# Channel attention of a normalised image batch: norms of queries and keys from weights times T on VectorE, summed by TensorE in fp32

## What is computed

```python
xt = gn(x).reshape(b, c, n).transpose(0, 2, 1)
q, k, v = split(xt @ w_qkv, 3, axis=-1)
q = q / max(sqrt(sum(q * q, over positions)), EPS)
k = k / max(sqrt(sum(k * k, over positions)), EPS) * temperature
attn = softmax(k^T q per head, axis=-1)
out = (v @ attn) @ w_out + b_out
result = x + out
```

## Time and profile before

| | us |
|---|---|
| median of 3 runs | 373.96 |
| profiled execution, its own time | 374.76 |
| span of that execution | 372.8 |
| TensorE busy | 331.2 (89%) |
| VectorE busy | 283.2 (76%) |
| ScalarE busy | 235.9 (63%) |
| POOL busy | 150.4 (40%) |

### The profile page before, as it was taken

The page is one execution under the profiler, slowest core; times in us unless marked ns, Lnnn a source line. Parts: engine busy times, 40 slices in busy tenths (PEclk is TensorE's granted clock), DMA queues, the critical chain, the costliest instruction groups (busy, mean ns, idle before and its releaser), DMA issues.

```text
span 372.8 us, 9327 instructions
## 1 busy us (share of the span) xinstructions
PE 331.2 (89%) x3724; PEld 233.4 (63%) x3724; DVE 283.2 (76%) x666; ACT 235.9 (63%) x410; POOL 150.4 (40%) x133
## 2 busy tenths in 40 slices
PE   0048856999999999999999999999999999999795
PEld 0036645875778566865777577856686577765452
DVE  4889855887699669986799769966998665359774
ACT  1098489763997299747996399729974699610200
POOL 0079858301970169203950197016920395001000
PEclk9999976899999999999999999999999999999999
DMA  7999900004994279815991499427981563034766
GB/s 235 359 286 246 244 16 3 2 2 139 300 323 132 86 233 326 247 44 137 336 335 44 134 297 338 124 87 226 320 261 45 165 217 88 2 105 150 230 213 192
DMA packets 30826, 67.73 MB, mean 182 GB/s; under 512 B 5504, under 2 KB 12096, under 8 KB 30784
## 3 DMA queue, kind: packets, MB, share of 16 engines
q1 hardware_dynamic: 30544, 66.56, 56.7%
q10 hardware_dynamic: 240, 0.59, 0.6%
HBM read 29.38 MB, written 28.31 MB: 155 GB/s over the span
## 4 chain that ended last, share of the span: by engine, by line
PE 64%; ACT 15%; issue 10%; DVE 5%; DMA 2%; SPq 2%; POOL 1%; ACTq 0%; POOLq 0%
PE u_ps L927 30%; PE g_ps L927 17%; PE s_ps L927 10%; ACT h_sb L543 4%; ACT tok L581 4%; ACT xn L537 3%; PE u_ps L976 2%; DMA wo<-in_L_conv_w_out_dram 2%; PE u_ps L977 2%; ACT h_sb L550 1%; DVE x_sb L855 1%; PE u_ps L979 1%; PE u_ps L978 1%; SPq L354 1%; SPq L359 1%
## 5 line engine op out<-in xcount | busy, mean ns | idle before, releaser
L474 POOL TENSOR_TENSOR l_sb<-xn,h_sb 128x768 f16<-128x768 f32 x63 | 103.8, 1649 | 56.0 <-ACT h_sb L543 55.7
L855 DVE SCALAR_TENSOR_TENSOR x_sb<-u_ps,bias,x_sb 128x384 f32<-128x384 f32 x144 | 85.9, 613 | 24.2 <-PE u_ps L927 24.1
L927 PE MATMUL g_ps<-tok 128*128 128x64 f16 (+1 forms) x864 | 87.1, 241 | 3.4 <-ACT tok L581 2.9
L537 ACT ACTIVATE xn<-x_sb,rb 128x768 f32<-128x768 f32 x63 | 63.6, 1020 | 29.7 <-POOL rb L486 29.7
L581 ACT COPY tok<-u_ps 128x384 f32<-128x384 f32 x144 | 65.0, 485 | 19.8 <-PE u_ps L979 18.6
L927 PEld LDWEIGHTS g_ps<-tok 128*128 128x128 f16 x864 | 57.0, 99 | 28.5 <-ACT tok L581 5.8
L728 DVE BATCH_NORM_STATS2 bnst<-x_sb 128x6 f32<-128x384 f32 x144 | 69.9, 543 | 5.3 <-DMA x_sb<-in_x_dram 5.2
L927 PE MATMUL u_ps<-h_sb,ml 128*128 128x384 f16 (+1 forms) x336 | 73.2, 327 | 0.0
L543 ACT ACTIVATE h_sb<-x_sb,rb 128x768 f16<-128x768 f32 x63 | 64.4, 1022 | 0.0
L976 PE MATMUL u_ps<-id,h_sb 128*128 128x128 f16 x288 | 48.9, 223 | 8.2 <-DVE l_sb L718 7.4
L977 PE MATMUL u_ps<-id,l_sb 128*128 128x128 f16 x288 | 48.9, 223 | 0.0
(11 more groups left out here) (144 smaller groups left out, 567.6 us busy)
## 6 DMA issues: line engine op xcount, KB each, us to landing
x_sb<-in_x_dram SPq DMA_DIRECT2D x48, 384.0 KB, 5.4
out_dram<-x_sb SPq DMA_DIRECT2D x48, 384.0 KB, 2.9
out_dram<-x_sb SPq DMA_DIRECT2D x48, 192.0 KB, 2.8
x_sb<-in_x_dram SPq DMA_DIRECT2D x45, 192.0 KB, 5.4
hl<-h_sb SPq DMA_DIRECT2D x48, 96.0 KB, 2.8
hl<-l_sb SPq DMA_DIRECT2D x48, 96.0 KB, 3.0
x_sb<-in_x_dram ACTq DMA_DIRECT2D x3, 192.0 KB, 4.2
w<-in_L_conv_w_qkv_dram SPq DMA_DIRECT2D x1, 288.0 KB, 7.4
```

The lines of the kernel that those rows point to most:

```text
L474: nc.gpsimd.tensor_tensor(l_sb[:, par, t, cols], xn[:, c % XN_RING, :], h_sb[:, par, t, cols], ALU.subtract).then_inc(l_ok, 1)
L537: nc.scalar.activation(xn[:, c % XN_RING, :], xcol(q, t, g * GW, GW), ACT.Identity, bias=rb[:, par, 1, t:t + 1], scale=rb[:, par, 0, t:t + ...
L855: V.scalar_tensor_tensor(out=xs, in0=block_ps(n), scalar=bias[:, t:t + 1], in1=xs, op0=ALU.add, op1=ALU.add).then_inc(out_ok, 1)
L927: return nc.tensor.matmul(dst, lhs, rhs, start=start, stop=stop, skip_group_check=True)
```

## The change

`scores` keeps only the products of 96 query columns of T with the key weights (24 products of 96 columns for a pair, in place of 24 of 192 and 24 of 96). `tq` holds the 192 query columns only. VectorE multiplies T, while it reads it for the low part, by the fp32 weights and 16, over all 384 columns, into the fp32 tile `pw`. A new step `squares` sums `pw` over its rows: 12 fp32 products, each with 96 columns of `pw` as the stationary operand and two columns of zeros and ones (`side`) as the moving one, into 8 columns of `s_ps` bank 0. `norms` on VectorE is one instruction on these 96 x 8 values. `scores` moves from block 12 to block 10 (in step 6 from 5 to 6), and on POOL `norm_power` moves from behind chunk 4 to behind chunk 2 (in step -1 behind chunk 3).

```diff
-PE_B = {0: ["gram"], 2: ["sums"], 4: ["w0"], 6: ["w1"], 12: ["scores"]}
+PE_B = {0: ["gram"], 2: ["sums"], 4: ["w0"], 6: ["w1"], 10: ["scores", "squares"]}
-POOL_B = ["power", 0, 1, 2, 3, 4, "norms", 5, 6, 7, 8]
+POOL_B = ["power", 0, 1, 2, "norms", 3, 4, 5, 6, 7, 8]
...
-FIRST_VEC_B = {0: ["gram", "var", "z", "t0", "t1"], 1: ["t2", "bn", "bn", "wo", "norms", "spread", "bn", "bn"]}
+FIRST_VEC_B = {0: ["gram", "var", "z", "wo", "t0", "t1"], 1: ["t2", "bn", "bn", "norms", "bn", "bn", "spread"]}
...
-                pool.wait_ge(diag, (q + 1) * DIAG)
+                pool.wait_ge(diag, q + 1)
...
-                nc.scalar.copy(tq[:, k, 0, :], src[:, 0:2 * C]).then_inc(th_ok, 1)
+                nc.scalar.copy(tq[:, k, 0, :], src[:, 0:C]).then_inc(th_ok, 1)
...
+                dve.wait_ge(n_mm, q + 1)
+                V.tensor_scalar(n8[:, :], n_ps, NORM_EPS ** 2 * NORM_FACTOR, None, ALU.max).then_inc(diag, 1)
...
-                ch = Chain(dve, diag, q * DIAG, DIAG)
-                V.tensor_tensor(dg[:, 4:8, :].rearrange("p (b j) c -> p b j c", b=2), qk_ps[:, :, :, 0, :], one, ALU.mult)
-                ch.then(V.tensor_tensor(dg[:, 0:4, :].rearrange("p (b j) c -> p b j c", b=2), kk_ps, one, ALU.mult))
-                ch.then(V.tensor_reduce(n8[:, :], dg[:, :, :], AX_X, ALU.add))
-                ch.then(V.tensor_scalar(n8[:, :], n8[:, :], NORM_EPS ** 2 * NORM_FACTOR, None, ALU.max))
...
-                V.tensor_tensor(tq[:, k, 1, :], src[:, 0:2 * C], tq[:, k, 0, :], ALU.subtract).then_inc(tl_ok, 1)
+                V.tensor_tensor(tq[:, k, 1, :], src[:, 0:C], tq[:, k, 0, :], ALU.subtract).then_inc(tl_ok, 1)
+                if k == 0:
+
+                    need(dve, n_mm, q)
+                V.scalar_tensor_tensor(out=pw[:, k, :], in0=src[:, 0:2 * C], scalar=W_SCALE, in1=(w1 if k == 2 else w0)[:, 0:2 * C],
+                                       op0=ALU.mult, op1=ALU.mult).then_inc(pw_ok, 1)
...
+            def squares(q):
+
+                pe.wait_ge(pw_ok, 3 * q + 3)
+                for a in range(4):
+                    c = C - C * (a // 2) + HC * (a % 2)
+                    terms = [(pw[:, k, c:c + HC], side[:, k, :]) for k in range(3)]
+                    dst = n_ps.rearrange("p (s b j) -> p s j b", s=2, b=2)[:, a // 2, a % 2, :]
+                    for k, (lhs, one) in enumerate(terms):
+                        last = mm(dst, lhs, one, k == 0, k == len(terms) - 1)
+                last.then_inc(n_mm, 1)
```

More of the change, by code:

```diff
@@ L69 @@
 PE_A = {0: ["flip"], 8: ["v"], 11: ["m"]}
-PE_B = {0: ["gram"], 2: ["sums"], 4: ["w0"], 6: ["w1"], 12: ["scores"]}
+PE_B = {0: ["gram"], 2: ["sums"], 4: ["w0"], 6: ["w1"], 10: ["scores", "squares"]}
 ACT_A = {0: ["h6"], 2: ["h7"], 4: ["x8"], 6: ["exp", "h8"], 11: ["v"], 14: ["m"]}
 ACT_B = ["x0", "t0", "t1", "t2", "h0", 1, 2, 3, 4, 5, "x6", "x7"]
-POOL_B = ["power", 0, 1, 2, 3, 4, "norms", 5, 6, 7, 8]
+POOL_B = ["power", 0, 1, 2, "norms", 3, 4, 5, 6, 7, 8]
 VEC_A = {0: ["soft_in"], 3: ["soft_out"], 7: ["v"], 11: ["m0"], 13: ["m1"], 17: ["stats"]}
-VEC_B = {0: ["gram"], 2: ["var"], 4: ["z"], 6: ["t0", "t1", "t2"], 12: ["norms"], 17: ["spread", "bn", "bn", "bn", "bn"]}
+VEC_B = {0: ["gram"], 2: ["var"], 4: ["z"], 6: ["t0", "t1", "t2"], 10: ["norms"], 17: ["spread", "bn", "bn", "bn", "bn"]}
 FIRST_PE_A = {14: ["wv"]}
-FIRST_PE_B = {0: ["gram", "sums"], 2: ["w0"], 7: ["w1", "scores"]}
+FIRST_PE_B = {0: ["gram", "sums"], 2: ["w0"], 7: ["w1", "scores", "squares"]}
 FIRST_ACT_A = {1: [6, 7], 2: [9], 3: [10], 4: [12], 5: [13], 6: [14]}
 FIRST_ACT_B = [0, "x1", "t0", "t1", "t2", "h1", 2, 3, 4, 5, "x6", "x7"]
-FIRST_POOL_B = ["power", 0, 1, 2, 3, 4, "norms", 5, 6, 7, 8]
+FIRST_POOL_B = ["power", 0, 1, 2, 3, "norms", 4, 5, 6, 7, 8]
 FIRST_VEC_A = {17: ["bn"] * 7 + ["stats", "wv"]}
-FIRST_VEC_B = {0: ["gram", "var", "z", "t0", "t1"], 1: ["t2", "bn", "bn", "wo", "norms", "spread", "bn", "bn"]}
+FIRST_VEC_B = {0: ["gram", "var", "z", "wo", "t0", "t1"], 1: ["t2", "bn", "bn", "norms", "bn", "bn", "spread"]}
 FIRST_BN = (0, 2, 2, 2, 1)
@@ L91 @@
 LAST_PE_A = {0: ["m"]}
-LAST_PE_B = {0: ["gram"], 2: ["w0"], 3: ["w1"], 5: ["scores"], 10: ["flip"], 16: ["v"]}
+LAST_PE_B = {0: ["gram"], 2: ["w0"], 3: ["w1"], 6: ["scores", "squares"], 10: ["flip"], 16: ["v"]}
 LAST_ACT_A = {0: ["m"]}
@@ L96 @@
 LAST_VEC_A = {0: ["m0", "m1"]}
-LAST_VEC_B = {0: ["gram"], 2: ["z"], 3: ["t0", "t1", "t2"], 5: ["norms"], 8: ["spread"], 10: ["soft_in"], 12: ["soft_out"],
-              15: ["v"]}
+LAST_VEC_B = {0: ["gram"], 2: ["z"], 3: ["t0", "t1", "t2"], 6: ["norms"], 8: ["spread"], 10: ["soft_in"], 12: ["soft_out"], 15: ["v"]}
 SUMS_AT = next(n for n, what in PE_B.items() if "sums" in what)
@@ L180, in preact_attention @@
         z16 = sb("z16", [P, 2, C], F16)
-        tq = sb("tq", [P, 3, 2, 2 * C], F16)
-        dg = sb("dg", [HC, 8, HC])
+        tq = sb("tq", [P, 3, 2, C], F16)
+        pw = sb("pw", [P, 3, 2 * C])
+        side = sb("side", [P, 3, 2])
         n8 = sb("n8", [HC, 8])
@@ L270, in preact_attention @@
         r8_ok = sem("r8_ok")
+        pw_ok = sem("pw_ok")
+        n_mm = sem("n_mm")
         diag = sem("diag")
@@ L287, in preact_attention @@
         out_ok = sem("out_ok")
-        STAT, GVAR, NORM, DIAG, SOFT, ATTN = 6, 4, 2, 3, 5, 6
+        STAT, GVAR, NORM, SOFT, ATTN = 6, 4, 2, 5, 6
         def high_count(k):
@@ L673, in _ @@
             V.memset(wl1[C1:P, :], 0.0)
+            ones = ((0, slice(0, P), 0), (1, slice(0, P), 1), (2, slice(0, C1), 0), (2, slice(C1, P), 1))
+            for k, rows, b in ones:
+                V.memset(side[rows, k, b:b + 1], 1.0)
+                V.memset(side[rows, k, 1 - b:2 - b], 0.0)
             for z in (wmh, wml):
@@ L985, in gram @@
                     need(pe, tl_ok, 3 * q)
-                    need(pe, diag, (q - 1) * DIAG + 1)
+                    need(pe, pw_ok, 3 * q)
                 first, end = j == 0, j == SLOTS - 1
@@ L1072, in scores @@
                         kc = slice(C + HC * j, C + HC * j + HC)
[L1073 to L1081, removed]
-                last.then_inc(s_mm, 1)
+                        terms = [(tq[:, b, 0, qc], wh0[:, kc]), (tq[:, b, 1, qc], wh0[:, kc]), (tq[:, b, 0, qc], wl0[:, kc]),
+                                 (tq[:, 2, 0, qc], wmh[:, b, kc]), (tq[:, 2, 1, qc], wmh[:, b, kc]),
+                                 (tq[:, 2, 0, qc], wml[:, b, kc])]
+                        for k, (lhs, w) in enumerate(terms):
+                            last = mm(qk_ps[:, b, j, :], lhs, w, k == 0, k == 5)
+                last.then_inc(s_mm, 1)
+            def squares(q):
[7 more added lines that the diff above has]
+                last.then_inc(n_mm, 1)
             def flip(q):
@@ L1166, in _ @@
             small_steps = {"gram": finish_gram, "w0": lambda q: gram_weights(q, False),
-                           "w1": lambda q: gram_weights(q, True), "scores": scores, "flip": flip,
+                           "w1": lambda q: gram_weights(q, True), "scores": scores, "squares": squares, "flip": flip,
                            "v": attn_values, "m": folded_weights}
```

9 lines of the change are left out of this document (4 added, 5 removed).

## The result

The changed kernel takes **387.74 us** (median of 4 runs, 385.82 to 388.97), the kernel before 373.82 us beside it (4 runs, 373.66 to 374.70): ratio 1.0372, 95% interval 1.0341 to 1.0403. Forecast were 373.1 us and a range from 370.0 to 378.2. The profiled execution took 388.12 us, with a span of 386.3.

The account below looks back on a forecast made before the run. Bound: ScalarE and TensorE in turn within each step, POOL feeding ScalarE. +0.3 (middle steps) +0.5 (step -1) -1.6 (last steps) = -0.8 us on 374.76; on the median 373.1 us, range 370.0 to 378.2.

Parts of the forecast that it names:

- TensorE's and POOL's parts: Middle steps: TensorE saves 1.0 us a pair, but POOL's earlier norm power delays ScalarE, so a step gains 0.
- The price of the squares: TensorE: an fp32 product taken at 0.085 us from the flips, 1.0 us for twelve; from above 0.34 each.
- tok0: ScalarE's copy of phase A's first transposed slot, where its chain meets TensorE's; 0.45 us of slack for TensorE's savings.
- The slow rival: fp32 products at 0.18 us each make POOL wait for the norms: sum +3.8, 377.8 us; chance 0.30.
- VectorE's and ScalarE's new durations: VectorE: low part 0.36 us, about 1 us less in sum; ScalarE: each copy of T about 0.16 us less.
- VectorE's products being free: VectorE's three products T x w, 1.65 us, cost no time because TensorE may run four blocks ahead.
- Step -1: Step without output blocks, TensorE at half clock: POOL's later chunk 4 delays tok0, +0.5 us.
- The last steps: Steps without ScalarE chunks: shorter scores and norms let flip and softmax start earlier, -1.6 us, at least -0.6.

Follow-up runs that it names:

- experiment 1: The kernel before with only scores and norms moved from behind block 12 to behind block 10, no fp32 product: 388.08 us, ratio 1.0365.
- experiment 3: The changed kernel with scores, squares and norms behind block 12 and POOL's list of the middle steps as before: 374.21 us, ratio 1.0013.
- 9: The changed kernel with ScalarE's wait for output block 11 moved from ahead of x3 to between x3 and h3: 383.72 us, ratio 1.0261.
- experiments 8: Experiment 3 with the scores alone behind block 10, squares staying behind block 12: 376.88 us, ratio 1.0096.
- experiment 10: The changed kernel with its squares in fp16 (pw and side in fp16): 376.23 us, ratio 1.0067.
- experiment 2: The changed kernel with scores, squares and norms behind block 11 in place of block 10: 379.99 us, ratio 1.0158.
- experiment 6: Experiment 5 with the squares in fp16 (pw and side in fp16): 368.34 us, ratio 0.9876.
- 5: Experiment 3 with POOL's list of step -1 as before too, norms behind chunk 4 in place of 3: 372.47 us, ratio 0.9977.
- experiments 4: The changed kernel with only POOL's list of the middle steps as before, norms behind chunk 4: 387.36 us, ratio 1.0357.
- experiment 7: Experiment 3 with all squares done twice, with the same result: 405.94 us, ratio 1.0876.

## Why the prediction was wrong, step by step

- **The step that failed** is in TensorE's and POOL's parts: "`scores` starts behind block 10, at 175.45, where block 11 begins now". I used this sentence to time the norms, and didn't ask who waits for block 11. Of ScalarE's chunks I looked only at x7, and the only chain that I let feed them was POOL's subtractions. ScalarE's wait at L571 was there to be read: the block that is pushed back is the last reader of rows that ScalarE overwrites. This is one mechanism, for six waits and, at 2.24 us a step, 13.4 of the 13.5 us between the spans; the two ends cancel (+0.9 and -0.9), which is luck. It is shown from both sides: made alone it costs all of it (experiment 1), removed it costs nothing (3), moved by one instruction it gives back 4 us (9), and its size follows how late block 11 ends. With 1.33, 1.83 and 3.43 us in experiments 8 and 10 and the changed kernel, less a slack of 0.47, come 0.86, 1.36 and 2.96, and x3 idles 0.80, 1.30 and 2.90; in experiment 1, with 3.31 and the whole 0.63, comes 2.68, and it idles 2.62. The sum is over the trace by 0.06 each time. (The 3.43 are 3.21 of scores and squares, 0.1 at the switch from the half tiles, and 0.12 because block 11 runs partly at 1.2 GHz; in the three steps without a slow stretch x3 idles 2.80.)
- **The price of the squares** was mis-sized: 0.085 us a product taken, 0.174 measured, in full clock; 3.82 us for twelve in step -1 at half clock. I took it from the flips, which are recorded as one instruction each; a product of the squares is recorded as two. TensorE saves nothing instead of 1.0 us. By an estimate even my own price would have cost: scores and squares of 2.1 us, less 0.63 of slack ahead of x3, less the 0.45 at tok0, is 1.0 us a step, +6 us over six. So the missed wait alone turns the sign, and the price adds to the size: at a quarter of it, experiment 10, +0.67 us a step are left.
- **The slow rival** had the price right (0.18 us from the 0.045 us of a narrow fp16 pass) but another path, norms, POOL, x7. On that path my own working gave 2.1 us for six steps (its terms, 176.53 + 2.16 + 0.4, put the norms at 179.1 and POOL 0.2 us late, not 179.2 and 0.35). In experiment 2, where it is alone, it costs 0.90 a step: POOL waited 1.08 us, since the squares there stand one block later. In the middle steps of the changed kernel it is hidden behind the longer wait; in step -1 it acts. The Trainium skill (FP8 and Floating Point Precision, TensorE Precision Notes) gives a true fp32 product four passes. In time the trace agrees: 0.174 us is close to four narrow fp16 products of 0.045. It records a product as two instruction pairs of 0.087 us, though, not four.
- **Right:** tok0 as the joint between ScalarE and TensorE, with half a us of slack for TensorE's savings (experiment 6: 1.5 us saved, 0.77 gained); VectorE's and ScalarE's new durations; VectorE's products being free (experiment 3 has them, and its period is 40.48).
- **Step -1** was forecast at +0.5 and came to +0.9 in the profiled execution (-0.7 and +1.6), with the squares at 3.82 us instead of 2.0 and POOL waiting 1.24 us for the norms, where I had it wait for nothing. Executions with the same step -1 differ by more than 0.9, so the agreement within half a us is partly luck. Putting the norms behind chunk 4 there is worth 1 to 1.7 us (3 against 5).
- **The last steps** were forecast at -1.6, at least -0.6 with dear squares. They gave -0.9 in the changed kernel and -0.7 in experiment 3; the flip lost its wait, as forecast:

```profile
354.28 0.53 PE L1102 MATMUL s_ps<-id,qk_s 96*96 96x96 f32 x4
```

## What to carry to other kernels

When work is put ahead of something on an engine's list, list every wait on what it delays, also the ones that are met early today: such a wait shows no idle in the profile, and its slack (here 0.63 us, the end of block 11 against the start of x3) must be worked out from two timelines. A buffer that is overwritten by parity makes the last reader of the old contents a deadline for the writer. And if an instruction in front of which a wait stands doesn't need it, the wait belongs behind it.

## What was not expected of the hardware

- An fp32 product with 96 stationary columns and two moving ones costs 0.17 us at 2.4 GHz (24 passes in 2.09 us here, in 2.03 in experiment 3, where full tiles follow) and 0.318 at 1.2 GHz (3.82 us for twelve); in fp16 it is 0.045 (experiment 10: twelve passes in 0.67 us, the last one's own 0.18 us among it). A moving side of two columns doesn't make it cheap.
- TensorE can fall to the 1.2 GHz level for over 3 us with no idle at all in front of it. With 24 two-column fp32 passes behind block 10 (changed kernel, experiments 4 and 9) 7 of 18 middle steps have such a stretch; with 48 of them (experiment 7) 5 of 6; with the 24 behind block 11 or 12 (experiments 2, 3, 5 and 8) none of 24, and none in experiment 1, which has no such pass. What decides it between equal steps, and why the place matters, stays open.
